# One-hot comparisons with the digits in PSUM, and gathers that keep step with the one-hot blocks

## The reference

```python
h = (x_flat @ W_gat).reshape(M, HEADS, NUM_EXPERTS)       # M nodes; 4096 here, 24 numbers each with the two scores
src = concatenate([edge_index[0], loops]); dst = concatenate([edge_index[1], loops])   # 262144 edges
e = leaky_relu(a_src[src] + a_dst[dst]); e_max = segment_max(e, dst)
ee = exp(e - e_max[dst]); denom = segment_sum(ee, dst)
msg = h[src] * (ee / (denom[dst] + 1e-16))[:, :, None]
agg = segment_sum(msg, dst) + b_gat
scores = layernorm(agg).mean over heads; topk_s, topk_i = top_k(scores, 2); w = softmax(topk_s)
out = sum over 4 experts of gate * (gelu(x @ W1[e] + b1[e]) @ W2[e] + b2[e])
```

## Time and profile before

| | us |
|---|---|
| median of 3 runs | 1025.7 (1022.24 to 1026.14) |
| the profiled execution | 1031.22 |
| its span in the trace | 1029.5 |

### The profile page before, as it was taken

One profiled execution on the slowest core, in us unless ns is written; L12 is line 12 of the kernel. 1 busy time (PEld: TensorE's weight loads), 2 busy tenths in 40 slices (PEclk: granted clock), 3 DMA queues, 4 the chain that ended last, 5 costly groups with the idle time before them and its releaser, 6 DMA issues.

```text
span 1029.5 us, 15298 instructions
## 1 busy us (share of the span) xinstructions
PE 644.5 (63%) x5984; PEld 331.3 (32%) x5984; DVE 762.1 (74%) x1477; ACT 306.7 (30%) x463; POOL 499.9 (49%) x399
## 2 busy tenths in 40 slices
PE   1501472499788888997787969999999410003421
PEld 1200130133333333333333445555656210002421
DVE  3999887697886877667888779998989831008775
ACT  1510350144554645444444431111111010000015
POOL 3990000017676766650000028888888877756000
PEclk9955875556987977669767969999999855555655
DMA  5010004100000000000000222000000000110001
GB/s 152 0 43 6 8 9 99 24 1 1 1 2 1 1 1 0 0 0 0 2 1 1 82 48 53 6 6 7 6 6 7 7 10 10 10 7 1 3 2 41
DMA packets 22001, 17.08 MB, mean 17 GB/s; under 512 B 13488, under 2 KB 18944, under 8 KB 21168
## 3 DMA queue, kind: packets, MB, share of 16 engines
q1 hardware_dynamic: 15424, 14.02, 5.1%
q0 software_dynamic: 5392, 2.18, 2.6%
q10 hardware_dynamic: 1120, 0.00, 0.1%
HBM read 10.51 MB, written 2.54 MB: 13 GB/s over the span
## 4 chain that ended last, share of the span: by engine, by line
PE 41%; DVE 30%; issue 13%; ACT 4%; SPq 2%; another core or an unknown queue 0%; DMA 0%; DVEq 0%; POOL 0%; ACTq 0%; POOLq 0%
PE psum L615 11%; PE psum L748 10%; DVE mx L1259 7%; PE psum L631 4%; DVE arena L1323 3%; PE psum L646 3%; PE psum L739 3%; PE psum L730 3%; SPq L381 2%; DVE arena L1289 2%; PE psum L598 2%; DVE arena L1030 2%; ACT arena L1004 1%; DVE arena L1026 1%; PE psum L669 1%
## 5 line engine op out<-in xcount | busy, mean ns | idle before, releaser
L493 POOL DMA_INDIRECT work<-node_rows,idx x160 | 257.8, 1611 | 53.1 <-issue 48.5
L1259 DVE TENSOR_REDUCE mx<-psum 128x2 f32<-128x512 f32 x256 | 164.3, 683 | 69.8 <-PE psum L631 67.9
L1323 DVE TENSOR_TENSOR arena<-arena 128x4096 bf16<-128x4096 bf16 (+1 forms) x128 | 182.0, 1486 | 18.1 <-PE psum L748 13.9
L915 ACT ACTIVATE arena<-psum 128x1024 f32<-128x1024 f32 x128 | 129.4, 1024 | 158.4 <-PE psum L646 158.4
L615 PE MATMUL psum<-arena 128*32 128x256 f32 x1024 | 168.3, 486 | 2.3 <-DVE arena L1299 1.4
L470 POOL TENSOR_SCALAR work<-arena,cF 128x184 f32<-128x184 f32 x128 | 93.7, 744 | 129.0 <-DVE arena L1159 73.2
L748 PE MATMUL psum<-arena 128*32 128x128 bf16 x2048 | 131.3, 420 | 4.3 <-DVE arena L1323 3.2
L631 PE MATMUL psum<-arena 32*128 32x256 bf16 x512 | 85.5, 340 | 27.5 <-DVE mx L1259 24.5
L748 PEld LDWEIGHTS psum<-arena 128*32 128x32 bf16 x2048 | 78.2, 149 | 43.6 <-DVE arena L1323 11.6
L615 PEld LDWEIGHTS psum<-arena 128*32 128x32 f32 x1024 | 56.8, 130 | 75.6 <-issue 57.8
L461 POOL COPY arena<-arena 128x160 f32<-128x160 f32 x16 | 5.4, 348 | 136.9 <-DVE arena L1145 91.7
(11 more groups left out here) (290 smaller groups left out, 989.7 us busy)
## 6 DMA issues: line engine op xcount, KB each, us to landing
work<-work SPq DMA_DIRECT2D x48, 64.0 KB, 2.0
work<-node_rows,idx POOLq DMA_INDIRECT x160
arena<-in_L_ffn_edge_index_dram SPq DMA_DIRECT2D x2, 1024.0 KB, 10.6
work<-edge_nodes SPq DMA_DIRECT2D x4, 368.0 KB
digits<-arena SPq DMA_DIRECT2D x1, 1024.0 KB, 4.0
arena<-digits SPq DMA_DIRECT2D x1, 1024.0 KB, 4.9
arena<-in_jpat_dram SPq DMA_DIRECT2D x1, 1024.0 KB, 6.8
out_dram<-work SPq DMA_DIRECT2D x4, 256.0 KB, 2.3
```

What stands on the lines that cost most here:

```text
L493: pool.indirect_dma_start(gath[:, l, :], None, tab, bass.IndirectOffsetOnAxis(ap=idx[:, l:l + 1], axis=0)).then_inc(done, 16)
L915: act.activation(pbuf[:, m % 4, :, :, :], ps[:, 2 + 2 * (m % 2):4 + 2 * (m % 2), :].rearrange("p j (k q) -> p j k q", k=U), ACT.Exp).then_ ...
L1259: v.reduce_max(mx[:, h, :], ps[:, h % 2, :].rearrange("p (u k) -> p u k", u=U), AX.X).then_inc(mx_done, 1)
L1323: ins = v.tensor_tensor(oh[:, buf, first:first + n, :], hl2[:, s_, bass.ds(blk * HC, HC)].rearrange("p (j c) -> p j c", j=1).broadcast_to( ...
```

## The change

The digits are brought from `hl2` in SBUF into PSUM by ScalarE, a quarter at a time: `stage_digits(i)` copies the digits of chunk `i`, as pairs of bf16 seen as fp32, into bank 4 or 5. The first two quarters are copied before the experts begin, the others at `m == 5` of chunks 1 and 2, when the quarter that lay in the bank before has been used. `one_hot_block` compares the constant in SBUF with the digits in PSUM, in bf16 as before, and waits at each chunk for `digits_staged`. All digits, and `jpat`, are raised by one (`DIG`), for which two casts on GpSimd become multiply-adds. In `gather`, before each even gather `l` from 2 to 128, GpSimd waits for `h_ready >= l // 2`: gathers `2k` and `2k + 1` wait until `k` blocks of one-hots are finished.

```diff
--- before.py
+++ after.py
@@ -46,6 +46,7 @@
 LT = CAP // 2
 NF = GF + 8
 HB, LB, HC = 128, 32, 32
+DIG = 1.0
 NBLK = EC // HC
 BIG = 1e30
 N_STORE = 4
@@ -78,7 +79,7 @@
             blocks.append(m)
     blocks.append(ident)
     cb = bf16_bits(np.concatenate(blocks, 1))
-    jpat = bf16_bits(np.tile(np.repeat(np.arange(HB), HC), (P, 1)))
+    jpat = bf16_bits(np.tile(np.repeat(DIG + np.arange(HB), HC), (P, 1)))
     return cf, cb, jpat
 
 
@@ -209,6 +210,9 @@
         jp = part2(8192, 2048, BF16).rearrange("p (j c) -> p j c", j=HB)
         hid = part2(10240, 2048).rearrange("p (n c) -> p n c", n=4)
         cnt = part2(12416, HB)
+        pdig = [psum[:, 4 + n, :].bitcast(BF16).rearrange("p (s c) -> p s c", s=2) for n in range(2)]
+        pdig_w = [psum[:, 4 + n, :].rearrange("p (s c) -> p s c", s=2) for n in range(2)]
+        hl2_w = part2(14880, EC).rearrange("p (s c) -> p s c", s=2)
         tns = part2(12544, CH)
         dcp = part2(8192, 3 * 1024 // 2, BF16).rearrange("p (t b q f) -> p t b q f", t=3, q=4, f=8)
         gone = sb("gone", [P, 4])
@@ -274,6 +278,7 @@
              "slots_ready", "slots_turned", "over_ready", "over_max", "idx_ready", "dl_turned", "dl_used", "hb_ready",
              "hb_done", "h_ready", "h_used", "cnt_done", "f1_ready", "hid_done", "f2_ready", "y_done"))
         hl_ready, hl_stored, hl_loaded = sem("digits_ready"), sem("digits_stored"), sem("digits_loaded")
+        digits_staged = sem("digits_staged")
         (seg_ready, ft_ready, ft_done, ex2_ready, lg_ready, lg_done, w_ready, sums_ready, mg_in, mg_out, gates_done,
          x2t_ready, final_done, oneh) = (sem(n) for n in (
              "seg_ready", "ft_ready", "ft_done", "ex2_ready", "lg_ready", "lg_done", "w_ready", "sums_ready", "merge_in",
@@ -429,8 +434,8 @@
 
                 gp.step(pool.tensor_scalar(ktmp, esf_, float(T - 1), 512.0, ALU.is_lt, ALU.mult))
                 pool.wait_ge(digits_split, 2)
-                gp.step(pool.tensor_copy(hl[:, 1, :], low))
-                gp.link(pool.tensor_copy(high.bitcast(F32), high))
+                gp.step(pool.tensor_scalar(hl[:, 1, :], low, 1.0, DIG, ALU.mult, ALU.add))
+                gp.link(pool.tensor_scalar(high.bitcast(F32), high, 1.0, DIG, ALU.mult, ALU.add))
                 pool.tensor_tensor(hl[:, 0, :], high.bitcast(F32), ktmp, ALU.add).then_inc(hl_ready, 1)
 
             edge_keys()
@@ -490,6 +495,8 @@
             def gather(first, last, done):
 
                 for l in range(first, last):
+                    if l % 2 == 0 and 2 <= l <= 2 * NBLK:
+                        pool.wait_ge(h_ready, l // 2)
                     pool.indirect_dma_start(gath[:, l, :], None, tab, bass.IndirectOffsetOnAxis(ap=idx[:, l:l + 1], axis=0)).then_inc(done, 16)
 
             pool.wait_ge(many_ready, 1)
@@ -950,6 +957,12 @@
 
             ybv = yb.rearrange("p (b u) e c -> p b u e c", u=U)
 
+            def stage_digits(i):
+
+                if i > 1:
+                    act.wait_ge(h_ready, 16 * (i - 1))
+                act.copy(pdig_w[i % 2], hl2_w[:, :, i * CH // 2:(i + 1) * CH // 2]).then_inc(digits_staged, 1)
+
             def expert_out(i, m):
                 act.wait_ge(f2_ready, 8 * i + m + 1)
                 act.copy(ybv[:, bass.ds(i * 4, 4), m % 2, m // 2, :], ps[:, 2 + m % 2, 0:4 * C].rearrange("p (t c) -> p t c", c=C)).then_inc(y_done, 1)
@@ -959,8 +972,13 @@
                     hidden(i, m)
                     if m:
                         expert_out(i, m - 1)
+                    if m == 5 and 1 <= i < NCH - 1:
+                        stage_digits(i + 1)
                 expert_out(i, 7)
 
+            act.wait_ge(hl_loaded, 16)
+            for i in range(2):
+                stage_digits(i)
             for i in range(NCH):
                 experts(i)
 
@@ -1319,10 +1337,13 @@
             def one_hot_block(blk, buf):
                 if later(blk, 1):
                     v.wait_ge(h_used, blk - 1)
+                if blk % 16 == 0:
+                    v.wait_ge(digits_staged, blk // 16 + 1)
+                here = slice(blk % 16 * HC, blk % 16 * HC + HC)
                 for s_, (first, n) in enumerate(((0, HB), (HB, LB))):
-                    ins = v.tensor_tensor(oh[:, buf, first:first + n, :],
-                                          hl2[:, s_, bass.ds(blk * HC, HC)].rearrange("p (j c) -> p j c", j=1).broadcast_to([P, n, HC]),
-                                          jp[:, 0:n, :], ALU.is_equal)
+                    ins = v.tensor_tensor(oh[:, buf, first:first + n, :], jp[:, 0:n, :],
+                                          pdig[blk // 16 % 2][:, s_, here].rearrange("p (j c) -> p j c", j=1).broadcast_to([P, n, HC]),
+                                          ALU.is_equal)
                     ins.then_inc((oneh, h_ready)[s_], 1)
 
             def chunk(i):
```

## The result

The changed kernel takes 993.27 us (median of 5 runs, 982.55 to 996.03) against 1025.7 (5 runs, 1022.24 to 1033.62): ratio 0.970, 95% interval 0.965 to 0.975, a gain of 3%, the medians 32.4 us apart. A ratio given with an interval counts only the runs within 1.5% of the fastest of their kernel, so it can differ from the quotient of two medians. The profiled execution is the lowest of its runs, 982.55, with a span of 981.0 against 1029.5. The earliest (late) had a granted clock of 0.77 up to there and TensorE busy for 391.5 us; the two latest (plain at 615.4, five_two at 615.6) had 0.70 and 0.72, and 421.5 and 417.9 us.

The account below looks back on a forecast made before the run. TensorE was taken to pace the stage, the last gather and 14.3 us behind it to set the end. Gathers freed gave -67 us, PSUM comparisons, ScalarE copies and digits nothing: 1025.7 - 67 = 959 us (945 to 972; whole range 945 to 1000).

Parts of the forecast that it names:

- a mild loss of supply: Stage: instruction supply stops while gather pairs run, 3.6 us per block instead of 3.1, +32 us, 991 us; chance 0.17.
- The comparison from PSUM costs nothing: Stage comparisons: bf16 from PSUM keeps 0.52 ns per element, 2.29 and 0.68 us; rival at 1.04 ns, chance 0.11.
- Gathers of 0.94 us, 128 by the last block, GpSimd's end 41 us after it: Stage and after: gathers run free, 32 remain behind the last block, GpSimd ends at 849.3 instead of 915.9, -66.6 us.
- the two SBUF inputs of VectorE: Stage: VectorE operations with two SBUF inputs, not its being busy, stretch gathers; 2283 ns mean there, 1005 ns afterwards.
- at 808.3 us as now: End of stage: the last block comes when it does now, with 128 gathers issued; no growth of the stage.
- the starved supply of instructions: Stage rival: unhindered gathers starve other engines; mild +32 us, 991 us, chance 0.17; severe beyond 1200 us, chance 0.04.
- the crawl of the earlier trace: Edge matmuls L790, behind the stage: a load and a matmul per 2.80 us while gathers run back to back.
- the gap of the earlier trace: Stage: after three 0.94 us gathers from 614.37, VectorE's next comparison comes at 617.91, after 4.06 us naming no engine.
- that the stream ran on for a while before it broke: Argument against starved supply: 3 us from 614.37 and 82 instructions at 854.70 ran before the break.
- If it then again drags until 14.3 us after GpSimd is through: Edge matmuls L790 end at 849.3 + 14.3 = 863.6, so the whole 66.6 us arrives; without drag, -79.
- That all behind L790 moves with it and keeps its length: Behind the edge matmuls: everything depends on L790 and the gathers; forecast length to the end 99.3 us, unchanged.
- 20 us of bias additions that are wanted after 1000 us: GpSimd's L504 and L510, queued behind the waits; taken as harmless because they are wanted only after 1000 us.

Follow-up runs that it names:

- late: Changed kernel with all gathers waiting for the last block, none beside the comparisons; 1109.59 us, stage 197.4 us.
- plain: Changed kernel without the waits, each indirect gather replaced by a plain transfer of 128 consecutive table rows, lookup left out; 946.16 us, stage 197.6 us.
- five_two: Changed kernel with five gathers in two blocks instead of four; 1032.84 us, stage 275.9 us.
- before: The kernel without the change; median 1025.7 us, stage 200.1 us in its profiled execution.
- after: The changed kernel in its profiled execution of 982.55 us, against a median of 993.27 us; stage 219.6 us.
- the four kernels of the same pace: The changed kernel run again unedited, and its three edits of where the bias additions lie, all two gathers per block; stages 222.1, 222.2, 223.1, 223.0 us.
- again: The changed kernel rerun with nothing edited; 990.59 us, stage 222.1 us.
- bias_later: Changed kernel with GpSimd's four bias additions held until VectorE has made both halves of the weights; 982.07 us.
- bias: Changed kernel with GpSimd's four bias additions waiting until VectorE's scans are done; 992.11 us.
- three_two: Changed kernel with three gathers in two blocks instead of four; 1011.85 us, stage 205.3 us.
- waitonly: The kernel before the change, comparisons from SBUF, with the 64 waits alone added; 1020.25 us, stage 200.3 us.
- The three bias runs: Changed kernel with bias additions held until the scans are done, held until the weights are made, or moved to VectorE; 992.11, 982.07, 977.89 us.
- four_burst: Changed kernel with four gathers back to back in every second block instead of two in each; 1015.59 us, stage 248.3 us.
- nopace: Changed kernel without the waits on finished blocks before the gathers; 1151.68 us, stage 407.2 us.

## Why the prediction was wrong

The time lies inside the whole range of 945 to 1000, but in the part that was given to a mild loss of supply with 0.17, and the forecast itself, 959, is 34 us too low. Some 18 of these show in the profiled executions and are explained below; the other 16 are the distance of those executions from their medians.

*The comparison from PSUM costs nothing*: right, 2290 and 678 ns, and the rate of two elements per cycle holds. By that the trace contradicts, for bf16 with one operand in PSUM, the perf-mode tier table of the Trainium skill, page "VectorE: DVE Perf Modes"; the same page's section "Why PSUM operands drop a tier" leaves such an operand the mode of two per cycle, and the trace agrees.

*Gathers of 0.94 us, 128 by the last block, GpSimd's end 41 us after it*: right but for 2.2 us, since two gathers behind the stage are still held, one of 2.46 us at 832.07 and one of 2.37 beside the SBUF-to-SBUF operation that is L1252 before, as the 2.36 of the earlier trace rows said. The prediction read these rows as "the two SBUF inputs of VectorE". That fits the comparisons, but not quite the two held here: L1252 has one tensor as input, and the gather at 832.07 lies at the start of L1267, the old L1249, which reads PSUM. Another of 2.37 us, at 811.33 in before, lies at the start of L1249 itself. What holds these stays open.

*"at 808.3 us as now"*: this step failed. It took the stage's length over, since nothing was added to TensorE or VectorE, but it grew by 19.5 us in after and by 22 to 23 in the four kernels of the same pace. The rival that named the cause, the starved supply of instructions, was there with 0.17, from the crawl of the earlier trace rows and the gap of the earlier trace rows. Its sizing, 0.5 us per block, 32 us in all, was 9 to 12 us too high: the measured growth is 0.30 to 0.36 per block. That its time, 991 us, lies so near the 993.27 is luck: the smaller growth, the scans and the shorter drag below, and the 16 us between medians and profiles happen to add up to it (959 + 19.5 + 7.3 - 7.6 + 2.2 - 3.5 + 16.2 = 993.1). What spoke against it in my text, that the stream ran on for a while before it broke and that GpSimd rests, was true as far as it went: the rests make the difference between 220 and 407 us. But a partial rest gives partial supply, and I took it for a full one. The evidence asked for a higher weight: in the one place where free gathers and running engines met, the supply had failed.

*"If it then again drags until 14.3 us after GpSimd is through"*: 6.8 us in after, 7.1 in again, and 4 of them are the 143 pairs still to do. The lag isn't fixed; it grows with the gathers behind the stage. From GpSimd's end to TensorE's full pace it is 2.7 us after 32 of them (2.9, 2.9 and 3.0 in again, bias_later and bias), 8.2 after 65 (three_two), 10.8 after 83 (before; 11.0 in waitonly) and 20.5 after 160 (late). This gave 7.6 us beyond the forecast.

*That all behind L790 moves with it and keeps its length*: failed as well, by 7.3 us. With L797 ending sooner after GpSimd, the scans came to lie fully beside the additions. I had noted those only as "20 us of bias additions that are wanted after 1000 us", not as a neighbour. Before already paid for such a meeting, 99.3 against the 90.4 of late; after pays 16. The three bias runs show this.

The sum in the profiled executions: -66.6 (gathers) + 2.2 (held gathers) - 7.6 (shorter drag) + 19.5 (stage) + 7.3 (scans) = -45.2, measured 376.3 - 421.3 = -45.0. The other 3.5 of the spans' 48.5 lie ahead of the stage. The medians are 32.4 us apart, 16.2 less than the two profiled executions (1031.22 - 982.55 = 48.7): that of before lay 5.5 above its median, that of after 10.7 below. What of this is the scatter ahead of the stage can't be told, since only the profiled executions show it.

## What to carry to other kernels

Unblocking an engine is not free if what it then does more of takes something from the others. Look in the trace for the place where the freed work already ran unhindered beside the busy engines, and price the gaps there, even when it is one place; then set its rate by trying three or four, since what the next unit costs on either side decides. Count there what it adds to the path and not how long it takes: the 32 gathers behind the stage take 43 us and cost 10. When a stretch moves, list what lands beside it anew, on GpSimd and VectorE above all: 20 us of additions that nobody waits for cost 8 us and more wherever VectorE's fp32 work lay.

## What the runs showed of the hardware

- Indirect gathers back to back (0.94 us, every 1.25) leave TensorE one load or matmul in 1.40 us, and 2 of VectorE's operations in 50; with 32 rows the standstill is the same as with 128. It outlasts the gathers, by 2.7 us after 32 of them and by 20.5 after 160. Plain transfers from the same engine, 95 in 50 us, leave them alone. Why the indirect form does it isn't settled: no run looks into how the instructions are fetched. The Trainium skill, page "Runtime: NRT & Kernel Launch", section "Instruction fetch mechanics", says that each engine streams its own instructions through a queue of its own and that the cost of going from one block of them to the next is mostly hidden. If what the gathers hold up is this fetching, nopace, at 6.73 us of TensorE's work in 50, is a case where it isn't hidden.
- Nor is it the SBUF interface that VectorE and GpSimd share: TensorE is hit as hard. That interface shows in the other direction, where gathers beside VectorE's two SBUF inputs take 1.89 us. The Trainium skill, page "SBUF — State Buffer", section "Who interferes with whom", has the rule of the two SBUF inputs, and the trace agrees. VectorE's fp32 scans and additions of 0.3 to 0.6 us, caught beside a GpSimd addition, last up to 4.9 us, as long as that addition.
- TensorE's granted clock falls behind the gaps: 0.98 over the stage in late and after, 0.90 in four_burst, 0.82 in five_two, with 191.4, 198.2, 213.0 and 224.8 us of busy time for the same matmuls.
- A late instruction is booked on whatever the engine waited for last: as "PE", "remote" or "issue". The sign is a start later than both the releaser's end and the engine's own last work, as at 627.98 above.
